# A transformer layer on one core: transposes of the weights moved behind the next scores, and the last product taken before its clip

## The reference, cut to what matters

```python
# for each row block: scores against 1601 context rows, masked
a = softmax(where(mask == 0, -2**15, Q @ K.T / sqrt(1024)))
x = x + (a @ V) @ Wo.T + bo                              # x2, the residual
x3 = layernorm(x, eps=1e-5)                              # the layer's own norm
xn = (x3 - mean) * rsqrt(var + 1e-3) * ln_gamma + ln_beta
beta = mean(abs(weight)); w_q = clip(round(weight / (beta + 1e-5)), -1, 1)
gamma = max(abs(xn))                                     # one number over all 2048 rows
xq = clip(xn * 128 / gamma, -128 + 1e-5, 128 - 1e-5)
out = x + (xq @ w_q) * (gamma * beta / 128)
```

## Time and profile before

| | us |
|---|---|
| median of three executions | 847.97 (847.71 to 848.97) |
| the profiled execution's own time | 847.01 |
| its span in the profile | 844.9 |
| PE busy in the span | 760.4 (90%) |
| DVE busy | 613.6 (73%) |
| ACT busy | 423.6 (50%) |
| POOL busy | 168.1 (20%) |

### The profile page before, as it was taken

One profiled execution on the slowest core, in us unless ns is written; L12 is line 12 of the kernel. 1 busy time (PEld: TensorE's weight loads), 2 busy tenths in 40 slices (PEclk: granted clock), 3 DMA queues, 4 the chain that ended last, 5 costly groups with the idle time before them and its releaser, 6 DMA issues. The chain is left out here.

```text
span 844.9 us, 12146 instructions
## 1 busy us (share of the span) xinstructions
PE 760.4 (90%) x4265; PEld 394.8 (47%) x4265; DVE 613.6 (73%) x1106; ACT 423.6 (50%) x871; POOL 168.1 (20%) x236
## 2 busy tenths in 40 slices
PE   8864888999999999999999979898689999999857
PEld 5441322333232332223333312785468888888746
DVE  5899687889988899998887620476046777777734
ACT  1552553776577766567778769221233323332331
POOL 2663000000000000000000000032405556655430
PEclk9996896999999999999999989999999999999988
DMA  7795411200000000000800000300012211222002
GB/s 212 214 271 170 103 51 38 64 26 26 2 1 2 2 1 2 1 1 14 278 2 1 1 2 1 110 1 0 1 39 79 78 55 61 78 78 78 1 0 100
DMA packets 27088, 47.32 MB, mean 56 GB/s; under 512 B 6048, under 2 KB 22944, under 8 KB 26272
## 3 DMA queue, kind: packets, MB, share of 16 engines
q1 hardware_dynamic: 25120, 43.94, 17.2%
q10 hardware_dynamic: 1920, 2.75, 1.1%
HBM read 38.16 MB, written 8.39 MB: 55 GB/s over the span
## 5 line engine op out<-in xcount | busy, mean ns | idle before, releaser
L486 DVE TENSOR_REDUCE part_max<-psum 128x1 f32<-128x512 f32 (+3 forms) x560 | 341.3, 668 | 54.6 <-PE psum L672 49.5
L591 ACT ACTIVATE probs<-psum 128x512 f32<-128x512 f32 (+3 forms) x640 | 293.7, 540 | 154.8 <-PE psum L697 153.8
L672 PE MATMUL psum<-k_stack,q_stack 96*128 96x512 bf16 (+4 forms) x640 | 214.8, 364 | 18.8 <-DVE psum L472 11.5
L697 PE MATMUL psum<-q_stack,k_stack 98*128 98x512 bf16 (+4 forms) x640 | 202.2, 357 | 13.1 <-DMA q_stack<-shift 11.3
L709 PE MATMUL psum<-probs,v_all 128*17 128x512 f32 (+3 forms) x1280 | 149.2, 538 | 0.3 <-PE psum L683 0.2
L672 PEld LDWEIGHTS psum<-k_stack,q_stack 96*128 96x128 bf16 (+1 forms) x640 | 60.1, 99 | 171.7 <-DVE part_max L486 121.0
L697 PEld LDWEIGHTS psum<-q_stack,k_stack 98*128 98x128 bf16 (+1 forms) x640 | 60.8, 99 | 94.2 <-ACT probs L591 39.2
L877 POOL MEMSET eps<- 128x4 f32 x1 | 0.1, 101 | 458.8 <-POOLq L273 458.8
L1392 PE MATMUL psum<-ctx_part,qc_part 128*128 128x512 f32 (+1 forms) x384 | 84.7, 371 | 5.0 <-POOL qc_part L1231 4.1
L1425 PE MATMUL psum<-v_parts,p_part 128*128 128x512 f32 (+3 forms) x416 | 76.8, 341 | 0.0
L1392 PEld LDWEIGHTS psum<-ctx_part,qc_part 128*128 128x128 f32 x384 | 67.3, 192 | 18.8 <-issue 4.9
(11 more groups left out here) (135 smaller groups left out, 674.6 us busy)
## 6 DMA issues: line engine op xcount, KB each, us to landing
mask<-in_mask SPq DMA_DIRECT2D x16, 800.5 KB, 4.3
pieces<-k_stack SPq DMA_DIRECT2D x24, 256.0 KB, 4.9
q_stack<-pieces SPq DMA_DIRECT2D x24, 256.0 KB, 4.2
k_stack<-pieces SPq DMA_DIRECT2D x24, 256.0 KB, 4.7
x_sb<-in_x SPq DMA_DIRECT2D x4, 512.0 KB, 8.8
out<-y SPq DMA_DIRECT2D x4, 512.0 KB, 2.9
q_stack<-in_ctxT SPq DMA_DIRECT2D x1, 1601.0 KB, 10.8
probs<-in_cos ACTq DMA_DIRECT2D x4, 256.0 KB
```

The lines of the kernel that those rows point to most:

```text
L486: nc.vector.tensor_reduce(part_max[:, h:h + m, r, c:c + 1], src, axis=AX_X, op=ALU.max).then_inc(m_read, 1)
L591: nc.scalar.activation(probs[:, s % 2, h, col:BLK], s_bank[h][:, col:BLK], ACT.Exp, scale=ATTN_SCALE).then_inc(exp_done, 1)
L672: last = nc.tensor.matmul(out, q_stack[b][0:rows, g * G + h, r * P:(r + 1) * P], k_stack[c][0:rows, g * G + h, 0:keys], start=True, stop=True)
L697: nc.tensor.matmul(s_bank[h][:, col:BLK], k_stack[s // TPB][0:rows, g * G + h, (s % TPB) * P:(s % TPB + 1) * P], q_stack[b][0:rows, g * G ...
```

## The change

In `cross`, TensorE's thirteenth transpose and the wait before it move behind the next tile's second score part. The last tile's `body` first transposes row blocks 0 and 1 of `x3`. ScalarE copies each transposed chunk twice, rounded to fp32r (`x3_high`) and in full (`x3_t`), and VectorE subtracts for the rest (`x3_low`). The product with the ternary weights is taken from unclipped, unscaled rows, as high and rest in fp32r, 64 products of 256 columns, 40 of them (`weigh_rows(0)` to `(4)`) ahead of the fourth row block's transposes. When the maximum is known, ScalarE computes what lies over the upper bound and VectorE what lies under the lower one, in bf16, and TensorE adds 64 bf16 products of these with minus the ternary weights (`take_excess`) into the same banks. The two factors gamma/128 and 128/gamma cancel, so the output needs only `beta`. POOL's scale takes three steps instead of seven, by (v(1 + 1e-3) + 1e-8)^-1/2. The last tile's gamma and beta are applied by VectorE (`last_rows`). Output goes in eight transfers of 256 KB, straight from x. `feed` and its block are gone. `x3_t`, `x3_low`, `over` and `under` lie in room that the stacks, `ctx_parts`, `e` and `mask` have left. The diff, cut to its core:

```diff
             nc.vector.tensor_tensor(w_tern[:, :, :], above[:, :, :], ffn_w[:, :, :], ALU.subtract).then_inc(tern_step, 1)
+            nc.vector.tensor_tensor(keep["minus_w"][:, :, :], ffn_w[:, :, :], above[:, :, :],
+                                    ALU.subtract).then_inc(tern_step, 1)
...
-    x3_t = keep["x3_t"]
+    x3_t, x3_high, w_tern, minus_w, ones = (keep[name] for name in ("x3_t", "x3_high", "w_tern", "minus_w", "ones"))
+    flat = [part[:, :, :].rearrange("p c s -> p (c s)") for part in ctx_parts]
+    x3_low = [flat[tb // 3][:, tb % 3 * EC * BLK:(tb % 3 + 1) * EC * BLK].rearrange("p (c t) -> p c t", c=EC)
+              for tb in range(NB)]
...
+    over, under = (tile[:, :, :].rearrange("p h s -> p (h s)").bitcast(BF16)[:, 0:NB * EC * BLK]
+                   .rearrange("p (b c t) -> p b c t", b=NB, c=EC) for tile in (e, mask))
...
-    x_bank = [[banks(psum, n) for n in pair] for pair in ((0, 1), (2, 3), (4, 5), (0, 1))]
+    x_bank = [[banks(psum, n) for n in pair] for pair in ((0, 1), (2, 3), (4, 5), (6, 7))]
+    UNITS = TILES // 2
+    out_bank = [banks(psum, u) for u in range(UNITS)]
+    top_row, top_all = banks(psum, 5)[0:1, 0:P], banks(psum, 5)[:, P:P + 1]
...
-    POOL_STEPS = 7
+    POOL_STEPS = 3
...
+            out = io["out"].rearrange("(u t p) e -> u p t e", p=P, t=2)
+            for u in range(UNITS):
+                sp.wait_ge(out_added, u + 1)
+                sp.dma_start(out[u], x[:, 2 * u:2 * u + 2, :]).then_inc(out_sent, 16)
+            sp.wait_ge(out_sent, 16 * UNITS)
...
-            for n, value in enumerate((LN_EPS, FFN_LN_EPS, -0.5)):
+            for n, value in enumerate((1.0 + FFN_LN_EPS, LN_EPS * FFN_LN_EPS, -0.5)):
...
                 pool.wait_ge(mv_done, i + 1)
                 n = i * POOL_STEPS
-                nc.gpsimd.tensor_tensor(va[:, :], mv[:, 1:2], consts[:, 0:1], ALU.add).then_inc(pool_step, 1)
+                nc.gpsimd.tensor_tensor(va[:, :], mv[:, 1:2], consts[:, 0:1], ALU.mult).then_inc(pool_step, 1)
                 pool.wait_ge(pool_step, n + 1)
-                nc.gpsimd.tensor_tensor(ra[:, :], va[:, :], consts[:, 2:3], ALU.pow).then_inc(pool_step, 1)
+                nc.gpsimd.tensor_tensor(vb[:, :], va[:, :], consts[:, 1:2], ALU.add).then_inc(pool_step, 1)
                 pool.wait_ge(pool_step, n + 2)
...
-                nc.gpsimd.tensor_tensor(scale[:, :], ra[:, :], rb[:, :], ALU.mult).then_inc(pool_step, 1)
+                nc.gpsimd.tensor_tensor(scale[:, :], vb[:, :], consts[:, 2:3], ALU.pow).then_inc(pool_step, 1)
...
             pairs(pool, body)
-            finish(TILES - 1)
...
+            def rest_of_rows(tb, c):
+                dve.wait_ge(x3_cut, tb * EC + c + 1)
+                dve.wait_ge(x3_copied, tb * EC + c + 1)
+                nc.vector.tensor_tensor(x3_low[tb][:, c, :], x3_t[:, tb, c, :], x3_high[:, tb, c, :].bitcast(F32),
+                                        ALU.subtract).then_inc(x3_rest, 1)
+            def last_rows():
+                i = TILES - 1
+                dve.wait_ge(z_done, i + 1)
+                dve.sem_inc(waits_met, 1)
+                nc.vector.tensor_tensor(z[:, :], z[:, :], gamma[:, :], ALU.mult).then_inc(last_row, 1)
+                dve.wait_ge(last_row, 1)
+                nc.vector.tensor_tensor(x3[:, i, :], z[:, :], beta[:, :], ALU.add).then_inc(last_row, 1)
+                dve.wait_ge(last_row, 2)
+                nc.vector.tensor_reduce(abs_max[:, i:i + 1], x3[:, i, :], axis=AX_X, op=ALU.max,
+                                        apply_absolute_value=True).then_inc(abs_done, 1)
+                dve.wait_ge(abs_done, TILES)
+                nc.vector.tensor_reduce(top[:, :], abs_max[:, :], axis=AX_X, op=ALU.max).then_inc(top_done, 1)
+            def lower_bound(tb):
+                dve.wait_ge(x3_copied, tb * EC + EC)
+                nc.vector.tensor_scalar(under[:, tb, :, :], x3_t[:, tb, :, :], bound[:, 0:1], 0.0,
+                                        ALU.add, ALU.min).then_inc(under_done, 1)
+            def add_out(u):
+                dve.wait_ge(out_ready, u + 1)
+                rows = x[:, 2 * u:2 * u + 2, :].rearrange("p t e -> p (t e)")
+                nc.vector.scalar_tensor_tensor(out=rows, in0=out_bank[u], scalar=keep["beta"][:, :], in1=rows,
+                                               op0=ALU.mult, op1=ALU.add).then_inc(out_added, 1)
...
+                if last:
+                    for tb in range(2):
+                        for c in range(EC):
+                            rest_of_rows(tb, c)
...
             pairs(dve, body)
+            for c in range(EC):
+                rest_of_rows(2, c)
+            largest(TILES - 2)
             scale_row(TILES - 1)
-            largest(TILES - 2)
-            largest(TILES - 1)
+            last_rows()
+            dve.wait_ge(top_turned, 1)
+            nc.vector.tensor_reduce(top_1[:, :], top_row, axis=AX_X, op=ALU.max).then_inc(top_found, 1)
+            rest_of_rows(NB - 1, 0)
+            dve.wait_ge(top_everywhere, 1)
+            for n in range(2):
+                nc.vector.tensor_scalar(bound[:, n:n + 1], top_all, (1 - 2 * n) * (QB - FFN_EPS) / QB, None,
+                                        ALU.mult).then_inc(bound_done, 1)
+            rest_of_rows(NB - 1, 1)
+            dve.wait_ge(bound_done, 2)
+            lower_bound(0)
+            lower_bound(1)
+            for tb in range(NB):
+                for u in range(2):
+                    add_out(2 * tb + u)
+                if tb + 2 < NB:
+                    lower_bound(tb + 2)
...
             for tb in range(NB):
                 for c in range(EC):
                     act.wait_ge(x3_turned, tb * EC + c + 1)
-                    nc.scalar.activation(x3_t[:, c, tb, :], x_bank[tb][c], ACT.Copy).then_inc(x3_copied, 1)
+                    nc.scalar.activation(x3_high[:, tb, c, :], x_bank[tb][c], ACT.Copy).then_inc(x3_cut, 1)
+                    nc.scalar.activation(x3_t[:, tb, c, :], x_bank[tb][c], ACT.Copy).then_inc(x3_copied, 1)
+            act.wait_ge(bound_done, 2)
+            act.wait_ge(x3_copied, NB * EC)
+            for tb in range(NB):
+                nc.scalar.activation(over[:, tb, :, :], x3_t[:, tb, :, :], ACT.Relu,
+                                     bias=bound[:, 1:2]).then_inc(over_done, 1)
...
+            def turn_rows(tb):
+                pe.wait_ge(xn3_done, min((tb + 1) * TPB, TILES - 1))
+                for c in range(EC):
+                    for k in range(TPB):
+                        last_x = nc.tensor.transpose(x_bank[tb][c][:, k * P:(k + 1) * P],
+                                                     x3[:, tb * TPB + k, c * P:(c + 1) * P], ident[:, :])
+                    last_x.then_inc(x3_turned, 1)
+            def weigh_rows(u):
+                tb = u // 2
+                pe.wait_ge(x3_rest, tb * EC + EC)
+                pe.wait_ge(x3_copied, tb * EC + EC)
+                for t in range(2):
+                    k = u % 2 * 2 + t
+                    for c in range(EC):
+                        for n, rows in enumerate((x3_high[:, tb, :, :], x3_low[tb])):
+                            nc.tensor.matmul(out_bank[u][:, t * E:(t + 1) * E], rows[:, c, k * P:(k + 1) * P],
+                                             w_tern[:, c, :], start=t == c == n == 0, stop=False)
+            def take_excess(u):
+                tb = u // 2
+                pe.wait_ge(over_done, tb + 1)
+                pe.wait_ge(under_done, tb + 1)
+                for t in range(2):
+                    k = u % 2 * 2 + t
+                    for c in range(EC):
+                        for n, rows in enumerate((over, under)):
+                            last_u = nc.tensor.matmul(out_bank[u][:, t * E:(t + 1) * E],
+                                                      rows[:, tb, c, k * P:(k + 1) * P], minus_w[:, c, :],
+                                                      start=False, stop=t == c == n == 1)
+                last_u.then_inc(out_ready, 1)
             def body(i, h, last):
                 if not last:
                     score(i + 1, 1 - h, 0)
 
-                pe.wait_ge(exp_done, i + 1)
-                for n, (j0, m) in enumerate(CHUNKS):
-                    if n == 3:
-
-                        pe.wait_ge(p_low, i * NCH + 1)
+                def turn_probs(n):
+                    j0, m = CHUNKS[n]
                     for j in range(j0, j0 + m):
                         keys = P if j < S2_TILES - 1 else S2_TAIL
                         last_t = nc.tensor.transpose(t_bank[n % 3][0:keys, (j - j0) * P:(j - j0 + 1) * P],
                                                      e[:, h, j * P:j * P + keys], ident[:, :])
                     last_t.then_inc(t_ready, 1)
+                if last:
+                    pe.wait_ge(e_taken, TILES)
+                    for tb in range(2):
+                        turn_rows(tb)
+                pe.wait_ge(exp_done, i + 1)
+                for n in range(3):
```

(76 more changed lines are left out.)

84 lines of the change are left out of this document (removed).

## The result

The changed kernel takes 824.59 us (median of four runs, 824.16 to 825.77), the kernel before beside it 847.84 (847.63 to 848.97): a ratio of 0.9725, with a 95% interval of 0.9708 to 0.9742. That is 23.3 us less. The profiled execution took 824.24 us, and its span is 822.5.

What follows compares the result with a forecast made beforehand. The steady loop was taken to be PE's, the end a chain of engines waiting for one another. 847.01 - 9.1 (gaps) - 0.3 (last tile) - 10.8 (end) = 826.8; the median, 0.96 above, gives 827.7 us, range 824.0 to 832.5.

Steps and rivals of the forecast that it cites:

- The gap of the thirteenth transpose: Steady loop: PE's gap before the thirteenth transpose goes, 0.65 us a tile, 9.1 us in fourteen tiles (7.6 to 9.8).
- The last tile: Last tile of the loop: `take` comes earlier than before and gives 0.3 us more.
- The chain through `take`: Loop, transpose to `exponential`: `take` at 4.4 us, next transposes possible at 10.4, 0.55 us left against PE's 10.94.
- the slower rival: Loop: slow hand-overs make the `take` chain the tile's length; slower overall from 12.3 us a tile; chance 0.02.
- The dear transpose: Loop: one more change between f32 transposes and fp32r products costs 0.3 to 0.65 us a tile, about 834; chance 0.12.
- ScalarE and VectorE at the end: End, from the last tile's first transpose: copies done at 7.0 us, last subtraction at 7.7, POOL's first step at 10.0.
- POOL's three steps: End: POOL's scale steps of 0.27, 0.27 and 0.55 us end at 11.1, and z starts at 11.4.
- PE before the fourth row block: End: PE is free at 13.5 us and sets the fourth row block's transposes, not the row, ready at 12.9.
- fp32r products: End: products of 256 columns take 0.14 us each (bounds 0.12 and 0.18); rival at 0.18 gives 830.3, within the range.
- The bf16 products: End: the 64 bf16 products of 256 columns take 0.11 us each.
- The end of the end: End: bounds at 16.1 us, last product 26.7, last addition 27.65, then 3.4 to the span's end at 31.0.
- The clock: End: rival that the clock falls to 1.2 GHz while the bounds are made, costing 2.5 us, 830.2; chance 0.15.

Runs made afterwards that it cites:

- The run with `over` alone: The changed kernel with the 32 products of `under` left out, while VectorE still makes all four pieces of `under`: 823.36 us.
- the kernel with PE busy at its end: The kernel before with filler transposes that nobody reads, ahead of the fourth row block's wait and behind the spread of the maximum: 846.28 us.

## Why the prediction was right, and where its sizes were off

The mechanisms held, and the time came out 3.1 us below the forecast. By the profiled executions the account closes within rounding: 826.8 forecast, 2.4 less in the loop, 1.3 less at the end, 0.4 less outside the span, 1.4 more for the first piece, against 824.24 measured. There is some luck in this. The two pieces that the change touches gave 11.8 + 12.1 = 23.9 us, where 20.2 were forecast and the range allowed for 23.9 at most. With the 0.4 outside the span they would put the time at 823.7, just under the low end; the first piece, 1.4 us longer in the profile, which no term of the forecast covers, brings it back.

- **The gap of the thirteenth transpose** is the term that was mis-sized most: 0.65 us a tile (0.54 to 0.70), measured 0.81 (11.62 to 10.81 in the mean over 14 tiles). The step that failed is the start of the scores, put 1.31 to 1.47 us after the first transpose. It is 1.23. The 0.109 us from one transpose's start to the next, worked out from the merged row, was right: in the rows above seven take 0.93 us and twelve 1.47. So the twelfth starts 11 times 0.109 = 1.20 us after the first. What was wrong is the step behind it: I gave the twelfth a full 0.109 before the scores as well, and they start 0.03 us after it. From 2.01 down to 1.23 are 0.78, and the charge behind the moved transpose is 0.06 instead of 0.08. That is 11.4 us in 14 tiles, not 9.1, and outside the bounds of 7.6 to 9.8.
- **The last tile** gives 0.4 (its interval is 10.32 instead of 10.70); forecast 0.3.
- **The chain through `take`** was right: forecast to start 4.4 us into the tile, it starts at 4.28; forecast to allow the next transposes at 10.4 us, the last tile, where PE waits for it, shows 10.32. PE's own 10.80 is only 0.48 more. So the slower rival, which decides at 12.3 us, is refuted, but the room is small.
- **The dear transpose** (834) is refuted by 0.06 us and by the period of 10.80.
- **ScalarE and VectorE at the end**, from the last tile's first transpose: copies done at 6.8 (7.0), last subtraction at 7.6 (7.7), POOL's first step at 9.74 (10.0).
- **POOL's three steps** took 1.82 us instead of 1.1. The forecast took durations of rows in which VectorE's subtraction has one source in PSUM. In the new end the first two steps lie beside a subtraction with both sources in SBUF. z is 0.2 late, since the rest was early.
- **PE before the fourth row block**: I said that PE would be free at 13.5 us and set the transposes. It is free at 12.5, and the row, ready at 13.05, sets them at 13.15. I sided with the wrong one of two that were 0.6 apart; the cost of that is nothing, but it means that z and POOL's steps are on the path, as seven steps and the subtraction from PSUM showed.
- **fp32r products** were taken at 0.14 us. They start (805.15 - 800.51) / 39 = 0.119 apart with the first's slow start in it, 0.117 without. The 0.12 worked out from the values' row was right, and I moved away from it for caution. The 24 late ones took 811.58 - 808.63 = 2.95 us, 0.123 each, where 3.4 was forecast: 0.4 us.
- **The bf16 products** start (818.71 - 817.08) / 15 = 0.109 us apart, as taken. The Trainium skill's rule ("TensorE: Matmul & The Clock Gate", section "Wait — 56ns, not 53.3ns?") gives 0.109 us for 256 columns; the trace agrees for bf16. For fp32r the runs have 0.117 to 0.123, between the rule and my value, so that the 1.3 us which the rule promised came to about 0.8: 0.4 in the late products, and 0.35 because the fourth row block's transposes start at 13.15 and not at 13.5.
- **The end of the end**: bounds at 15.8 (16.1), last product ends at 26.2 (26.7), last addition at 27.0 (27.65), and the last transfer, 256 KB, takes 2.7 us and not 3.4. End at 29.75 instead of 31.0.
- **`under`** is 0.74 (0.75), and PE's wait for it is there but short: the last 16 products start 0.35 us behind the one before (816.73 to 817.08), where 0.109 is usual. The run with `over` alone showed how near DVE is.
- **`minus_w`** costs nothing: the first instruction of `cross` starts 1.42 us later than before, exactly as late as `fold` had started.
- **The clock** kept full speed in the profile, as forecast. But it fell in one of four profiles with the same waits (0.59 and 0.56 over four us, 1.4 us of time: up to the products behind the bounds that end runs as the changed kernel's, 15.8 and 15.9 us). The chance of 0.15 that I gave to it was for the median; it would better have been told as a cost in some executions.

## What to carry to other kernels

When a transpose or product waits for an engine that clears its bank, put the next independent products before it, and price the gap by the start of the following instruction in a row of the same kind, not by the end of a merged row. When work can be taken ahead of a global maximum, what it brings is counted twice: once as work out of the tail, once as the clock that TensorE keeps through the wait. And after such an edit look for the next idle stretch that it makes at the last tile: here the moved order alone made the end 1.3 us longer.

## What the runs showed that I had not expected

**POOL and VectorE held each other up.** Beside VectorE's subtraction with both sources in SBUF, POOL's steps on one value per partition took 0.59 and 0.52 us instead of 0.19, its 256-wide addition 1.08 instead of 0.74, and the subtraction itself up to 1.23 instead of 0.69. The occurrences of the subtraction in the changed kernel, by line (shortest, median and longest in ns):

```profile
L1313 DVE TENSOR_TENSOR ctx_part<-q_stack,x_high x8: 679/692/1233, 796.9 to 808.7; 128x512 fp32r<-128x512 f32 x8
```

With one source in PSUM, all of it was gone, and nothing else was edited. The Trainium skill has this as a rule ("SBUF — State Buffer", section "Who interferes with whom"): a VectorE instruction with two SBUF inputs contends with a GpSimd instruction that reads SBUF, over shared ports that it calls an exclusive lock, where the order of issue decides which is blocked. The trace agrees: `va` starts at 802.49 beside a subtraction that began at 802.33 and takes 0.69 us, and it ends at 803.08, 0.06 us after it. I hadn't weighed that rule in the prediction; it would have added 0.7 us to POOL's steps.

**The clock fell behind a wait no longer than others.** Waits of 1.58 us and 1.59 (the kernel with PE busy at its end) before the last tile's transposes left it at full speed; 2.16 us in the same place brought it to 0.50. Near the bounds the same three short waits left it alone in three profiles and not in the fourth. What decides there stays open.
